# Transformer block on one core: order of the even units' first projections, spacing of the last unit's blocks, order of the last rests

## The reference

```python
x = x + layernorm(attention(layernorm(x)))        # q, k, v = x @ w.T ; softmax(q k / 4) v ; @ w_o.T
x = x + layernorm(ffn(layernorm(x)))
# ffn: xr = mu_r*x + (1-mu_r)*x_prev ; xk = mu_k*x + (1-mu_k)*x_prev      (x_prev: the token before)
#      out = sigmoid(xr @ W_r.T) * (relu(xk @ W_k.T)**2 @ W_v.T)
```

## Time and profile before

| | |
|---|---|
| median of 3 executions | 1284.59 us (1283.14, 1284.59, 1287.94) |
| the profiled execution, its own time | 1282.99 us |
| its span, first to last instruction | 1281.2 us, so 1.8 us lie around it |
| busy: TensorE, ScalarE, VectorE, GpSimd | 98%, 83%, 61%, 21% |
| mean granted TensorE clock | 0.998 |

### The profile page before, as it was taken

The page is one execution under the profiler, slowest core; times in us unless marked ns, Lnnn a source line. Parts: engine busy times, 40 slices in busy tenths (PEclk is TensorE's granted clock), DMA queues, the critical chain, the costliest instruction groups (busy, mean ns, idle before and its releaser), DMA issues.

```text
span 1281.2 us, 25644 instructions
## 1 busy us (share of the span) xinstructions
PE 1258.9 (98%) x10684; PEld 606.2 (47%) x10684; DVE 786.1 (61%) x1736; ACT 1064.4 (83%) x1153; POOL 269.5 (21%) x351
## 2 busy tenths in 40 slices
PE   8999999999999999999999999999999999999997
PEld 5544444444444444444544444444444445534345
DVE  6653746748465773847567584666747466463747
ACT  3688888888888888888888888888888888898962
POOL 1000112222211321212221221223222122222211
PEclk9999999999999999999999999999999999999999
DMA  4365563316612185124933166321761129300001
GB/s 152 97 148 167 100 130 83 100 51 127 118 54 83 51 176 106 34 67 102 146 84 91 45 110 131 72 84 51 152 113 49 36 78 171 84 1 30 5 1 34
DMA packets 61798, 112.72 MB, mean 88 GB/s; under 512 B 6512, under 2 KB 31344, under 8 KB 61616
## 3 DMA queue, kind: packets, MB, share of 16 engines
q1 hardware_dynamic: 61360, 109.60, 37.7%
q10 hardware_dynamic: 288, 1.05, 0.3%
HBM read 68.42 MB, written 41.94 MB: 86 GB/s over the span
## 4 chain that ended last, share of the span: by engine, by line
PE 90%; DVE 6%; ACT 2%; issue 1%; POOL 1%; DMA 1%; ACTq 0%; DVEq 0%
PE O L603 37%; PE S L584 25%; PE M L350 14%; PE M L337 11%; PE M L247 2%; ACT PT L591 2%; DVE sth L700 1%; DVE A L709 1%; PE M L487 1%; DMA A<-w_dram 1%; DVE mvh L702 0%; POOL rsh L705 0%; DVE xnT L413 0%; DVE xB L735 0%; DVE xnT L375 0%
## 5 line engine op out<-in xcount | busy, mean ns | idle before, releaser
L591 ACT ACTIVATE PT<-S 128x1024 f32<-128x1024 f32 x1024 | 1003.5, 1025 | 162.2 <-PE S L584 161.8
L603 PE MATMUL O<-PT,V 128*17 128x512 f32 x4096 | 538.9, 598 | 0.0
L584 PE MATMUL S<-QS,KS 50*128 50x512 f32 x2048 | 464.6, 450 | 3.9 <-ACT PT L591 3.9
L584 PEld LDWEIGHTS S<-QS,KS 50*128 50x128 f32 x2048 | 211.1, 183 | 452.5 <-ACT PT L591 373.2
L603 PEld LDWEIGHTS O<-PT,V 128*17 128x17 f32 x4096 | 67.8, 95 | 139.7 <-issue 137.9
L704 POOL TENSOR_SCALAR veh<-mvh 128x2 f32<-128x2 f32 x96 | 22.4, 233 | 495.9 <-DVE mvh L702 494.2
L913 DVE SCALAR_TENSOR_TENSOR A<-Z,M 128x512 f32<-128x512 f32 x30 | 20.4, 681 | 160.5 <-PE M L350 160.5
L337 PE MATMUL M<-xnT,WH 64*128 64x512 f32 x512 | 112.3, 395 | 3.2 <-DVE xnT L413 3.2
L350 PE MATMUL M<-WH,cT 64*128 64x256 f32 (+1 forms) x496 | 83.2, 281 | 2.8 <-DVE rec L660 2.8
L350 PE MATMUL M<-WH,xnT 64*128 64x256 f32 x512 | 84.7, 278 | 0.3 <-DVE xnT L413 0.3
L350 PE MATMUL M<-WH,B 64*128 64x256 f32 (+1 forms) x496 | 81.5, 278 | 0.0
(11 more groups left out here) (129 smaller groups left out, 1617.0 us busy)
## 6 DMA issues: line engine op xcount, KB each, us to landing
scr<-p SPq DMA_DIRECT2D x124, 256.0 KB
QS<-scr SPq DMA_DIRECT2D x56, 256.0 KB, 6.0
KS<-scr SPq DMA_DIRECT2D x56, 256.0 KB, 11.0
QS<-scr SPq DMA_DIRECT2D x70, 128.0 KB, 5.8
KS<-scr SPq DMA_DIRECT2D x68, 128.0 KB, 8.0
xA<-x_dram SPq DMA_DIRECT2D x16, 512.0 KB, 7.4
xB<-x_dram SPq DMA_DIRECT2D x16, 512.0 KB, 5.2
out_dram<-xB SPq DMA_DIRECT2D x15, 512.0 KB, 3.0
```

What stands on the lines that cost most here:

```text
L584: fn = lambda e, p=p, a=a, rows=rows: e.matmul(PS[p][:, a, :], KS[qd][rows, p, kt * 128:kt * 128 + 128], QS[qd][rows, p, hf * 512:hf * 512 ...
L591: e_fn = lambda e, p=p: e.activation(PT[i % 2][:, 2 * p:2 * p + 2, :], PS[p][:, :, :], ACT.Exp, scale=SCALE)
L603: fn = lambda e, j=j: e.matmul(PO[32 * j:32 * j + 17, :], V[b % 2][:, kt, 4 * qd + j, :], PT[i % 2][:, j, :], start=(kt == 0), stop=(kt == 7))
```

## The change

Three edits. In `EVEN`, K00 stands directly behind Q00 and ahead of T10. In the last unit (u = 15) `age` is 2 only for s < 5 and 1 from there; in unit 14 it stays 2 for s < 20. After the last step's quad has been put into `resting`, it is moved from the last to the first place of that list.

```diff
@@ values
             quad_done[b, qd] = pv_of[i]
             if kt == 7:
                 until_rest(quad(g, qd))
+                if i == len(steps) - 1:
+                    resting.insert(0, resting.pop())
@@
-        EVEN = "W3 T00 T01 y0 y1 Q00 T10 K00 T11 z0 z1 k0 k1 r0 r1 v0 v1 Q01 K01"
+        EVEN = "W3 T00 T01 y0 y1 Q00 K00 T10 T11 z0 z1 k0 k1 r0 r1 v0 v1 Q01 K01"
@@ main loop
-                age = 2 if b + 1 == B and s < 20 else 1
+                age = 2 if b + 1 == B and s < (5 if hf else 20) else 1
```

## The result

| | before | after |
|---|---|---|
| median of 20 executions | 1286.03 us | 1281.73 us (1279.70 to 1284.17) |
| ratio | 1 | 0.9968, 95% interval 0.9959 to 0.9976 |
| profiled execution, its span | 1281.2 us | 1278.2 us |

A forecast was written before the change was run, and what follows sets the result against it. TensorE, 98% busy, was taken to bound the kernel. Terms of -4.6 (Edit 1), +2.6 (Edit 2), -3.85 and -0.44 (the end) gave -6.3 us from 1283.9: 1277.6 us, range 1274.8 to 1282.2.

The forecast's parts named there:

- Edit 1: Even units 2 to 12: K00 ahead of T10 removes its bank wait, 0.76 us each in six units, 4.6 us.
- The cover of T11: Even units: the copy that frees T11's bank ends before its transposes start, by 0.4 to 1.8 us, taken as 1.1.
- Edit 2: Last unit: age 1 from step 5 delays T0 by 2.6 us (2.3 to 3.0).
- T0: Start of the `values` of step 31 in unit 15, 1239.49 us before the change; forecast to move 2.6 us later.
- The wait of k0: Last unit: k0 waits for GpSimd to complete C, 1.1 to 1.4 us, taken as 1.25, the middle.
- The remainder: Last unit: 0.4 us of T0's delay, for ScalarE's later On between bare steps.
- Edit 3 and the end: After the last step: T at T0 + 1.8, 3.85 us less; full clock and y0, y1 give 0.44 us more.
- The base: Starting time for the forecast: 1283.9 us, middle of four executions of the kernel before, 0.7 below the given median.
- No wait for C: Last unit: k0's wait does not arise, T0 + 1.3 only; total -7.6 us, 1276.3; chance 0.12.
- Filler gap: End: idle time before z0 grows to 1.0 us and the clock falls there; total -4.6 us, 1279.3; chance 0.10.
- Wait of edit 1 only moves: Even units: T11 or z0 waits for VectorE as long as K00 did; total -1.7 us, 1282.2; chance 0.13.
- Clock in the row of four turns: Steps 12 to 15 of six units: clock falls during transposes; total +3.9 us, 1287.8; chance 0.05.

The follow-up runs named there:

- e8: Changed kernel with two filler matmuls ahead of the loop and the mix continued before the quad in step 16 of the last unit; 1277.33 us, ratio 0.9932.
- e13: Kernel before with three filler matmuls of 0.9 us in TensorE's idle times at the start; median 1283.96 us, ratio 0.9980.
- e14: Changed kernel with three filler matmuls of 0.9 us in TensorE's idle times at the start; median 1277.59 us, ratio 0.9932.
- e7: Changed kernel with the mix's second rest continued ahead of the quad's in step 16 of the last unit; ratio 0.9957.
- e1: Kernel before with only K00 moved ahead of T10; ratio 0.9964.
- e10b: Kernel before, unchanged, profiled and timed again; 1283.29 us.
- e12b: Kernel before, unchanged, profiled and timed once more; 1282.94 us.
- e2: Kernel before with only the age change in the last unit and the quad moved to first place; ratio 0.9987.
- e3: Kernel before with only the age change in the last unit; ratio 1.0012.
- e4: Kernel before with only the last step's quad moved to first place in `resting`; ratio 0.9994.
- e15: Changed kernel with three start fillers, plus the mix ahead of the quad in step 16 of the last unit; median 1276.84 us, ratio 0.9928.

## Why the prediction was right or wrong

**Edit 1: right.** Six waits of K00, all gone; 0.73 us each (13.77 against 14.50 in unit 6) instead of 0.76. The cover of T11 was 1.2 us, forecast 1.1.

**Edit 2: right, with its terms off against each other.** T0 moved by 2.6. The wait of k0 was 0.94 us instead of 1.25, and z0's 0.16 instead of 0.25. For k0 the reason shows: the product CC of the quad took 0.42 us, not 0.70, now that it no longer ran beside GpSimd's first subtraction for C (1206.68 to 1207.97 before, 1204.31 to 1205.59 after). My 4.65 to 4.93 had that difference as its bounds, and I took the middle. VectorE before, then after:

```profile
1207.54 0.70 DVE L630 TENSOR_TENSOR CC<-T,rec 128x256 f32<-128x256 f32 x1
```

```profile
1205.91 0.42 DVE L632 TENSOR_TENSOR CC<-T,rec 128x256 f32<-128x256 f32 x1
```

The remainder, which I had put down to ScalarE with 0.4, was 0.8 (2.6 less 0.7, 0.94 and 0.16; the 0.7 itself was not measured apart). Of it, 0.36 lie in z0's step: 2.93 us long against 2.41 before, less its wait of 0.16. The rest was not traced.

**Edit 3 and the end: right.** T at T0 + 1.72 (forecast 1.8), y0 after 0.40 us of idle time (0.5), clock 1.00, the last instruction 37.3 us after T0 (37.4).

**The base: wrong.** The failed step is "I take 1283.9 - 6.3", with no term for the start and "about 1.5 us from a median of few executions" as its spread. That start is not a constant: with the start of either kernel the clock falls between 36 and 44 us in some executions, which put the first On copy 1.6 to 3.5 us late in the profiles that had it, and in e8 it fell at 8 to 12 us, for 2.1 us. The four times of before whose middle I took, 1282.99 to 1287.94, were very likely such a mixture already (one was profiled, with a clean start), and I read them as noise about a middle. The measured 1281.73 lies 4.1 us above the forecast: 2.1 because the base came out at 1286.03 and not 1283.9, and 2.0 because the difference was 4.3 and not 6.3. A clean execution of the changed kernel takes 1276.85 us and one of before 1282.94 to 1283.29, so 1277.6 is nearly a clean execution's time, while the median of 20 contains mostly unclean ones. None of the first 20 spans of the changed kernel was below 1277.2, while 1275.1 and 1275.2 are its clean ones; its median lay 4.9 us above its clean time, that of before about 2.9. Those 2.0 us are what was missing of the 6.1. That the clock of the start is the whole of it is shown by e13 and e14; that the first 20 executions of the changed kernel had so few clean starts was not in any forecast of mine, and whether that was luck is open.

**The rivals.** No wait for C: false, it was 0.94 us; e7 shows its price. Filler gap: it grew to 0.92 us (1.0 worked out), and the clock stayed at 1.00 from 1256 to 1264. Wait of edit 1 only moves: false. Clock in the row of four turns: false, it stayed at 1.00 (522 to 533 us, unit 6 of the kernel after). The Trainium skill, "TensorE: Matmul & The Clock Gate", Part 4 on the PE-mode transpose, says that transposes do not count as busy in the way matmuls do. Here the four transposes of a step take 0.66 us of 2.23 to 2.30, scores and values most of the rest, and no run had transposes alone, so this trace neither bears it out nor refutes it.

**What stays open.** Why the clean start was seen less often with edit 1. I count a span as clean within 1.3 us of the shortest that its stretches allow. The changed kernel had it in 0 of the first 20 executions and 2 of 7 later ones, e1 in 0 of 8, e7 in 1 of 6: 3 of 41. With the list of before it came in 12 of the 74 timed beside the experiments (spans 1280.7 to 1282.0), in e10b and e12b, and in 2, 0 and 5 of 10 in e2, e3 and e4: 21 of 106. The start's instructions are the same. A difference as large comes by chance about once in twelve times, if the executions are independent, so it is not settled. e14 shows only that without the falls the edits lose nothing. Nor was it tried which of the two loop-side fillers does the work.

## What to carry to other kernels

Where executions of one kernel scatter in groups, find the groups' places before forecasting a difference: the mean clock beside each span, and the time of the first fixed event in each profile, tell them. Time two kernels from such an event, or fill the idle times first, or a real 6 us shows as 4 in one comparison and nearly 7 in the next. In a kernel bound by TensorE, look for a wait that repeats once per unit; moving one piece removed it at no cost, while work that was started earlier at the end paid back 2.6 of the 4.4 us that it won.

## What the runs showed of the hardware

TensorE's clock fell between 36 and 44 us (0.57, mostly the 1.2 GHz level) after idle times of 0.95 and 0.89 us in some executions and not in others of the same instructions, and in e8 between 5 and 15 us (0.83); e3 kept full clock after 3.03 us of idle time, where before lost it after 2.76. The length of a single idle time did not decide it there. At the wait for the weights the one fall came with the longest wait of all profiles, 2.01 us (e8); none came after 0.37 to 1.71 us. Two or three filler matmuls of about 0.9 us in such places put the first On copy at 61.36 to 61.57 us where a clean start had 61.22 to 61.36, and the spread of spans went from 6.4 us to 2.0, 0.5 and 2.7 (e13, e14, e15). The same VectorE product (CC, 128x256) took 0.42 us or 0.70 us: in the profile of before 29 of its 63 took 0.7, all with GpSimd busy for 0.41 to 0.44 us of them, and the other 34 had it busy for 0.20 us at most.
